# One core, a gated convolution and a mixture of experts: router logits computed with the operands swapped, and the statistics for a median measured and spread in another order

## The chip, the core and the metric

The kernel runs on one core of a Trainium2 chip. The metric is device time in microseconds (us), from one execution to the next of the same program. The engines are named as the profile names them: PE (TensorE, matmuls) with PEld (its weight loads), DVE (VectorE), ACT (ScalarE), POOL (GpSimd) and SP (SyncE, which only issues DMAs here). Each runs its own instructions in order, and they meet at semaphores.

## The reference, cut to what matters

The input is 8 images of 512 channels and 16 x 16 pixels, that is 2048 tokens of 512 channels.

```python
def conv(x):                                   # x: channel layer norm of the input, b c (h w)
    mean, mx, std = x.mean(-1), x.max(-1), x.std(-1, ddof=1)
    u = stack([mean, mx, std], -1)             # 8 x 512 x 3
    med = median(u.reshape(b, -1))             # one median of 1536 values for each image
    z = einsum('bck,ck->bc', (u - med)**3, cfc_w) / sqrt(1 + eps) * bn_w + bn_b
    return x * sigmoid(z)[:, :, None, None]
x = x + conv(ln_c(x))
def ffn(x):                                    # x: layer norm of a token
    logits = x @ router_w.T                    # 8 experts, the best one is taken
    top, idx = top_k(logits, 1)
    return sigmoid(top) * glu(x, w1[idx], v1[idx], w2[idx]) + glu(x, shared weights)
t = t + ffn(ln_t(t))
```

Every product is f32 and is made of three matmuls of type fp32r: each operand is split into a HI part and the rest, LO, and HI x HI, HI x LO and LO x HI are added.

## The kernel before, in words

**The stages.** (1) Up to about 41 us the 8 images ("batches" in the code, 256 tokens each) are normalized and turned so that channels lie on partitions; the turned batch `b` lies in two banks of the PSUM tile `GU`, two channel groups (k = 0, 1) in the first bank and two (k = 2, 3) in the second. Mean, maximum and standard deviation over its tokens are taken there: DVE measures the first bank with `bn_stats` and `bn_aggr` (L685, L693) and takes both maxima (L694, L696), ACT sums and squares the second bank (L513, L517), POOL makes the standard deviations (L391 to L394). (2) From 41 to 63 us the medians are found: the statistics are copied 16-fold into `scratch` (DVE L713 eight of twelve columns, ACT L537 four), turned by 12 transposes on PE (L1097) and one more (L1099) so that 1536 values of an image stand on each of its 16 partitions, and searched in 7 steps (L725 on DVE, L546 on ACT, each counting one half of the values; PE adds the counts). Before its first step ACT splits four pieces of the first weights (L532). Between the steps PE runs matmuls on ones, whose results nobody reads (L1071). (3) From 63 to 76 us the gates are made and applied to the first tiles. (4) From 76 to 203 us the 16 tiles of 128 tokens pass through the shared expert while the next tiles are prepared. (5) The tokens are sorted by expert, gathered and sent through the experts in blocks of 128.

**The loop of stage 4.** Its order is written out by hand: `PREPARED` names the tiles that each step n prepares (one, or two in steps 3 and 6). A step of PE is: gate product of tile n+1 (12 matmuls of 512 columns), transposes of the hidden tile n (L1148), up product of n+1, transposes of the next tile (`prepare`, L1141), down product of tile n into `yb`, routing of the prepared tile (L1187). Routing loads the tile's 128 x 128 HI and LO pieces as weights, eight in all, and moves the 16 columns of `router_parts` (HI and LO of 8 experts) through each; the logits of 128 tokens come out in `th` with tokens on partitions, and DVE copies them out (`keep_logits`, L806). `th` also holds the transposes of the hidden tile, so the two uses wait for one another. After the last tile DVE picks the experts (`choose`, L891 on).

**What the names are.** `means_kept`, `std_done`, `bank_measured`, `squares`, `spread_ready` and `spread_act` are the semaphores between stages 1 and 2. `y_used` tells that DVE has read `yb`. `xhi`, `xlo`, `hhi`, `hlo` tell that HI and LO of a turned tile are written. `SPLIT_AFTER` names the steps after which a third of the next weights is split (ACT L490, DVE L831).

Of the kernel before, what the change touches and what calls it, by code (L numbers as in the profile page):

```python
# [44 lines left out]
def program(nc, B, x_tok, conv_par, router, weights, xn_d, z_d, out):  # L45
# [12 lines left out]
    with ExitStack() as ctx:  # L58
# [36 lines left out]
        steps = sb("steps", [P, SEARCH_STEPS])  # L95
        conv = sb("conv", [P, KC * 5])
# [109 lines left out]
        logits = sem("logits")  # L206
        logits_used = sem("logits_used")
# [20 lines left out]

        def tally(i):

            return (yb, mb)[i % 2][:, i:i + 1]
# [10 lines left out]
        def stats_columns(of, to):  # L242

            return stats_rows[:, :, of:to].rearrange("p b s -> p s b").unsqueeze(3).to_broadcast([P, to - of, B, TPART])
# [92 lines left out]
        def _(pool):  # L337
# [50 lines left out]
            def channel_std(b):  # L388
# [3 lines left out]
                pool.wait_ge(bank_measured, 2 * b + 1)  # L392
# [95 lines left out]
        def _(act):  # L488
# [48 lines left out]
            act.activation(spread_rows(BY_COPY, KC * 3), stats_columns(BY_COPY, KC * 3), ACT.Copy).then_inc(spread_act, 1)  # L537
# [50 lines left out]
            silu_gate(0, 0)  # L588
            x_hi(2, 2)
            for n in range(NT - 1):  # L590
# [6 lines left out]
                for t in soon:  # L597
                    if t >= RING:
                        norm_a(t, t % RING)
                for t in now[1:]:  # L600
                    x_hi(t, t % RING)
                if n in SPLIT_AFTER:
                    k = SPLIT_AFTER.index(n)
                    act.wait_ge(w_in[k], 16 * 2)
                    split_hi(w_raw[:, k, :, :], w_parts[:, 1, k, HI, :, :])
            x_hi(NT, 0)
# [35 lines left out]
        def _(dve):  # L642
# [30 lines left out]

            def measure(tokens, channels):


                if tokens is not None:
                    dve.wait_ge(x_in[tokens], 16)
                    for h in range(2):
                        note(dve.bn_stats(bn_parts[:, h, :], x_sb[:, 2 * tokens + h, :]))  # L680
                if channels is not None:
                    aT = GU[:, 2 * (channels % 2):2 * (channels % 2) + 2, :].rearrange("p a (h t) -> p a h t", t=TPB)
                    dve.wait_ge(aT_ready, channels + 1)
                    for k in range(2):
                        note(dve.bn_stats(bn_parts[:, 2 + k, :], aT[:, 0, k, :]))  # L685
                settle()
                if tokens is not None:
                    for h in range(2):
                        note(dve.bn_aggr(tok_mv[:, 2 * tokens + h, :], bn_parts[:, h, :]))
                    dve.engine_nop().then_inc(stats_a, 1)  # L690
                if channels is not None:
                    for k in range(2):
                        note(dve.bn_aggr(stats[:, channels, k, 0:2], bn_parts[:, 2 + k, :]))  # L693
                    dve.tensor_reduce(stats[:, channels, 0:2, MAX], aT[:, 0, :, :], AX_X, ALU.max).then_inc(bank_measured, 1)  # L694
                    dve.wait_ge(squares, 2 * (channels + 1))
                    dve.tensor_reduce(stats[:, channels, 2:4, MAX], aT[:, 1, :, :], AX_X, ALU.max).then_inc(bank_measured, 1)  # L696
# [107 lines left out]
            def keep_logits(t, u):  # L804
                dve.wait_ge(logits, t + 1)
                dve.tensor_copy(logit_parts[:, t, :] if isinstance(t, int) else tile_of(logit_parts, t), th[:, 0:2 * E]).then_inc(logits_used, 1)  # L806
# [34 lines left out]
            keep_logits(0, 0)  # L841
            gated(0, 0)
            x_lo(2, 2)
            keep_logits(1, 1)
            for n, prepared in enumerate(PREPARED):
# [5 lines left out]
                norm_tile(first, first % RING)  # L851
                h_lo(n, n % 2)
# [4 lines left out]
                for t in held:  # L857
                    keep_logits(t, t % RING)
# [5 lines left out]
                keep_logits(first, first % RING)  # L864
# [24 lines left out]
            def choose():  # L889

                dve.wait_ge(logits_used, NT)  # L891
# [117 lines left out]
            n = len(PREPARED)  # L1009
            choose()  # L1010
# [54 lines left out]
        def _(pe):  # L1065
# [32 lines left out]

            pe.transpose(V[:, NV - BY_ACT:NV - BY_ACT + P], stats_rows[:, :, :].rearrange("p b r -> p (b r)"), ident[:, :]).then_inc(v_ready, 1)  # L1099
# [62 lines left out]
            def gate_product(n, slot, parity, q, before):  # L1162
# [3 lines left out]
                product(gu(parity, GATE), xT[:, slot], q, GATE).then_inc(g_done, 1)  # L1166
# [11 lines left out]
            def route(t, slot):  # L1178
# [4 lines left out]
                else:  # L1183
                    pe.wait_ge(logits_used, t)
# [24 lines left out]
            for n, prepared in enumerate(PREPARED):  # L1209
# [3 lines left out]
                pe.wait_ge(logits_used, first - len(held))  # L1213
# [36 lines left out]
            gate_product(n + 1, 0, 0, 0, 0)  # L1250
# [88 lines left out]
```

## Time and profile before

| | us |
|---|---|
| three runs | 424.27, 425.77, 425.97 (median 425.77) |
| the profiled execution | 425.56 |
| its span, first to last instruction | 423.6 |
| PE busy in the span | 385.3 (91%) |
| DVE, ACT, POOL busy | 258.9, 160.1, 135.2 |

The span is the time from the first to the last instruction on the trace; 1.96 us of the execution lie outside it. PE's busy share is an average: from 76 us on it is busy nearly all the time, before that it mostly waits.

### The profile page before, as it was taken

How to read it: one execution, taken by the hardware profiler on the slowest of the kernel's cores; microseconds unless marked ns; L12 is line 12 of the kernel's file. 1: busy time of each engine (PE TensorE's matmuls, PEld its weight loads, DVE VectorE, ACT ScalarE, POOL GpSimd, SP SyncE). 2: the span in 40 equal slices, each digit the busy share in tenths (PEclk: the TensorE clock that was granted, in tenths of full speed). 3: DMA queues.
4: the chain of work that ended last, by engine and by line, in shares of the span. 5: the costliest groups of instructions: out<-in, count | busy, mean ns of one | idle time of the engine just before them, and what ended most of it. 6: DMA issues, size and time to landing. Idle time of an engine off the chain costs nothing.

```text
span 423.6 us, 6668 instructions
## 1 busy us (share of the span) xinstructions
PE 385.3 (91%) x1920; PEld 313.0 (74%) x1921; DVE 258.9 (61%) x493; ACT 160.1 (38%) x265; POOL 135.2 (32%) x187
## 2 busy tenths in 40 slices
PE   1556766999999999999999999999999999999995
PEld 1444224888888888888888888888888888888883
DVE  5896776555584795575775557627546753776322
ACT  3887764122323522322112335435153634353210
POOL 6676841001010000003212034633425452345301
PEclk9999799999999999999999999999999999999999
DMA  7900221011121363122004085765626775652210
GB/s 287 406 5 2 99 100 50 26 50 51 50 76 50 107 216 150 51 91 108 26 26 124 26 319 193 262 230 195 231 84 256 258 241 190 233 197 71 74 45 29
DMA packets 15788, 55.96 MB, mean 132 GB/s; under 512 B 2575, under 2 KB 2575, under 8 KB 12304
## 3 DMA queue, kind: packets, MB, share of 16 engines
q1 hardware_dynamic: 10960, 40.93, 27.1%
q0 software_dynamic: 4800, 14.69, 9.7%
q8 instruction: 15, 0.25, 0.2%
q14 instruction: 13, 0.11, 0.1%
HBM read 43.02 MB, written 13.63 MB: 134 GB/s over the span
## 4 chain that ended last, share of the span: by engine, by line
PE 84%; DVE 6%; ACT 3%; issue 3%; POOL 2%; DMA 1%; DVEq 0%; POOLq 0%; ACTq 0%
PE GU L1156 47%; PE yb L1156 23%; PE th L1148 4%; PE tx L1141 4%; PE th L1187 3%; DVE search_junk L725 2%; DVE bn_parts L680 1%; ACT tiles L502 1%; POOL tok_rstd L385 1%; DMA x_sb<-x_tok 1%; PE mb L1156 1%; ACT scratch L513 1%; PE th L1071 1%; DVE bn_parts L685 1%; PE th L1134 1%
## 5 line engine op out<-in xcount | busy, mean ns | idle before, releaser
L1156 PE MATMUL GU<-w_parts,xT 128*128 (+1 forms) x864 | 213.8, 396 | 0.0
L1156 PEld LDWEIGHTS GU<-w_parts,xT 128*128 128x128 f32 x864 | 158.5, 188 | 32.0 <-issue 0.2
L1156 PE MATMUL yb<-w_parts,hT 128*128 (+1 forms) x420 | 102.7, 393 | 0.0
L573 ACT ACTIVATE hT<-th 128x512 fp32r<-128x512 f32 x36 | 21.6, 599 | 190.2 <-PE th L1148 190.2
L1156 PEld LDWEIGHTS yb<-w_parts,hT 128*128 128x128 f32 x420 | 77.8, 188 | 15.7
L440 POOL DMA_INDIRECT out<-x_sb,scatidx x20 | 37.3, 1865 | 92.8 <-DVE x_sb L1006 87.5
L831 DVE TENSOR_TENSOR w_parts<-w_raw,w_parts 128x2048 f32 (+1 forms) x24 | 54.9, 2288 | 6.8 <-issue 6.5
L816 DVE TENSOR_TENSOR hidden<-hidden,GU 128x512 f32<-128x512 f32 x36 | 24.8, 688 | 42.2 <-PE GU L1156 37.0
L490 ACT ACTIVATE w_parts<-w_raw 128x2048 f32 (+1 forms) x24 | 45.2, 1910 | 4.2 <-issue 4.1
L414 POOL TENSOR_TENSOR x_rstd<-x_mv,eps 128x1 f32<-128x1 f32 x16 | 3.3, 205 | 118.7 <-DVE x_mv L792 118.7
L810 DVE TENSOR_TENSOR hT<-th,hT 128x512 fp32r<-128x512 f32 x36 | 24.8, 688 | 24.5 <-ACT hT L573 24.5
L563 ACT ACTIVATE xT<-tx 128x512 fp32r<-128x512 f32 x36 | 21.4, 595 | 34.5 <-PE tx L1141 34.5
L1083 PE MATMUL GU<-ident,tiles 128*128 128x128 f32 x64 | 15.3, 423 | 20.7 <-ACT tiles L502 20.7
L1006 DVE SCALAR_TENSOR_TENSOR x_sb<-yb,slotinfo,x_sb 128x512 f32<-128x512 f32 x19 | 14.2, 749 | 26.5 <-PE yb L1156 23.7
L1083 PEld LDWEIGHTS GU<-ident,tiles 128*128 128x128 f32 x64 | 12.7, 224 | 22.6 <-issue 16.0
L435 POOL DMA_INDIRECT x_sb<-z_d,tokidx x20 | 19.5, 974 | 26.0 <-DMA z_d<-x_sb 20.2
L801 DVE TENSOR_TENSOR xT<-tx,xT 128x512 fp32r<-128x512 f32 x36 | 24.6, 683 | 4.2 <-ACT xT L563 4.2
L431 POOL DMA_INDIRECT tiles<-xn_d,tokidx x20 | 19.3, 964 | 22.3 <-DVE slotinfo L958 16.5
L1141 PE MATMUL tx<-ident,tiles 128*128 128x128 f32 x144 | 21.6, 273 | 2.0 <-DVE xT L801 2.0
L568 ACT ACTIVATE hidden<-GU 128x512 f32<-128x512 f32 x36 | 21.6, 600 | 2.1 <-PE GU L1156 2.1
L1148 PE MATMUL th<-ident,hidden 128*128 128x128 f32 x144 | 21.5, 272 | 0.0
L1148 PEld LDWEIGHTS th<-ident,hidden 128*128 128x128 f32 x144 | 17.8, 140 | 4.6
(203 smaller groups left out, 352.7 us busy)
## 6 DMA issues: line engine op xcount, KB each, us to landing
w_raw<-weights SPq DMA_DIRECT2D x27, 1024.0 KB, 5.4
x_sb<-x_tok SPq DMA_DIRECT2D x8, 512.0 KB, 7.4
xn_d<-tiles SPq DMA_DIRECT2D x16, 256.0 KB, 2.0
z_d<-x_sb SPq DMA_DIRECT2D x16, 256.0 KB, 2.0
tiles<-xn_d,tokidx POOLq DMA_INDIRECT x20, 4.5
x_sb<-z_d,tokidx POOLq DMA_INDIRECT x20, 5.3
out<-x_sb,scatidx POOLq DMA_INDIRECT x20, 7.4
conv<-conv_par SPq DMA_DIRECT2D x1, 10.0 KB, 9.9
```

What stands on the lines that cost most here:

```text
L440: pool.indirect_dma_start(out[:, :], rows(scatidx, b), zg[:, b % RING, :], None, bounds_check=T - 1, oob_is_err=False).then_inc(o_out[b % ...
L490: act.activation(hi, raw, ACT.Copy).then_inc(whi, 1)
L568: act.activation(hidden[:, parity, :], gu(parity, GATE), ACT.Silu).then_inc(silu, 1)
L573: act.activation(hT[:, parity, HI, :, :], th[:, :].rearrange("p (k t) -> p k t", k=KC), ACT.Copy).then_inc(hhi, 1)
L801: dve.tensor_tensor(xT[:, slot, LO, :, :], tx[:, :].rearrange("p (k t) -> p k t", k=KC), xT[:, slot, HI, :, :].bitcast(F32), ALU.subtract) ...
L810: dve.tensor_tensor(hT[:, parity, LO, :, :], th[:, :].rearrange("p (k t) -> p k t", k=KC), hT[:, parity, HI, :, :].bitcast(F32), ALU.subtr ...
L816: dve.tensor_tensor(hidden[:, parity, :], hidden[:, parity, :], gu(parity, UP), ALU.mult).then_inc(hid_ready, 1)
L831: dve.tensor_tensor(lo, w_raw[:, k, :, :], hi.bitcast(F32), ALU.subtract).then_inc(wlo, 1)
L1083: last = pe.transpose(aT[:, k, h * P:(h + 1) * P], tiles[:, t % RING, k * P:(k + 1) * P], ident[:, :])
L1141: last = pe.transpose(tx[:, k * P:(k + 1) * P], src[:, k * P:(k + 1) * P], ident[:, :])
L1148: last = pe.transpose(th[:, k * P:(k + 1) * P], hidden[:, parity, k * P:(k + 1) * P], ident[:, :])
L1156: last = pe.matmul(dst, left[:, lp, kc, :], wset(q, k, wp, kc), start=(i == 0), stop=(i == 3 * KC - 1))
```

## The change

It has two parts that do not touch one another.

**Routing swapped.** Now `router_parts` (16 columns) is the weight and the tile's piece, 128 columns, is moved through it. The logits come out in `th` with the 16 (expert, part) rows on partitions and tokens along the columns. ACT copies these 16 x 128 values to `logits_T` (two slots of SBUF), PE transposes them back to 128 x 16 into `yb` in the next step (`turn_logits`; the last one into `tx`, in the middle of a gate product), and DVE takes all tiles of a step with one copy (`take_logits`). In the diff, `keep_logits` is a function of ACT's program now, `take_logits` one of DVE's.

```diff
+        logits_T = search_junk[0:2 * E, 0:2 * P].rearrange("p (a c) -> p a c", a=2)
...
-                        last = pe.matmul(th[:, 0:2 * E], xT[:, slot, lp, kc, :], router_parts[:, kc, :, :].rearrange("p h e -> p (h e)"),
+                        last = pe.matmul(th[0:2 * E, 0:P], router_parts[:, kc, :, :].rearrange("p h e -> p (h e)"), xT[:, slot, lp, kc, :],
...
+            def turn_logits(n, bank):
+                for i, t in enumerate(routed_in(n - 1)):
+                    pe.wait_ge(logits_kept, t + 1)
+                    pe.transpose(bank[:, i * 2 * E:(i + 1) * 2 * E], logits_T[:, t % 2, :], ident[0:2 * E, 0:2 * E]).then_inc(logits_turned, 1)
...
                 gate_product(n + 1, (n + 1) % RING, (n + 1) % 2, 0, 0)
-                pe.wait_ge(logits_used, first - len(held))
+                if n:
+                    pe.wait_ge(y_used, n)
+                turn_logits(n, yb)
                 transpose_h(n, n % 2)
...
+                pe.wait_ge(logits_used, n + 1)
                 down_product(n, n % 2, 0, 0)
...
-            gate_product(n + 1, 0, 0, 0, 0)
-            pe.wait_ge(logits_used, NT)
+            gate_product(n + 1, 0, 0, 0, 0, lambda: turn_logits(n, tx))
...
+            def keep_logits(t):
+                act.wait_ge(logits, t + 1)
+                act.activation(logits_T[:, t % 2, :], th[0:2 * E, 0:P], ACT.Copy).then_inc(logits_kept, 1)
...
+            def take_logits(n, bank):
+                tiles_in = routed_in(n - 1)
+                first, many = tiles_in[0], len(tiles_in)
+                dve.wait_ge(logits_turned, tiles_in[-1] + 1)
+                dve.tensor_copy(logit_parts[:, first:first + many, :],
+                                bank[:, 0:many * 2 * E].rearrange("p (t e) -> p t e", t=many)).then_inc(logits_used, 1)
...
                 norm_tile(first, first % RING)
+                take_logits(n, yb)
                 h_lo(n, n % 2)
```

On PE, one step of the loop of stage 4 (step 1), before:

```order
L1187 MATMUL th<-router_parts,xT 128x16 x8
L1156 MATMUL GU<-w_parts,xT 128x512 x12
L1148 MATMUL th<-ident,hidden 128x128 x4
L1156 MATMUL GU<-w_parts,xT 128x512 x12
L1141 MATMUL tx<-ident,tiles 128x128 x4
L1156 MATMUL yb<-w_parts,hT 128x512 x12
```

and the same step now (`search_junk` is the memory in which `logits_T` lies):

```order
L1232 MATMUL th<-xT,router_parts 16x128 x8
L1201 MATMUL GU<-w_parts,xT 128x512 x12
L1240 MATMUL yb<-ident,search_junk 128x16
L1193 MATMUL th<-ident,hidden 128x128 x4
L1201 MATMUL GU<-w_parts,xT 128x512 x12
L1186 MATMUL tx<-ident,tiles 128x128 x4
L1201 MATMUL yb<-w_parts,hT 128x512 x12
```

The eight routing matmuls stand where they stood, now writing 16 x 128, and one small transpose per tile has come in ahead of the transposes of the hidden tile. Steps that route two tiles have two.

**The last two batches by bank, and the spread by kind.** For batches 6 and 7 DVE now measures the first bank of both and only then takes the maxima of the second banks, which wait for ACT's squares. The spread is by kind: the four maxima (DVE), the four means (DVE), the four standard deviations (ACT), and PE transposes in that order; it waits for the standard deviations only ahead of the last transpose.

```diff
-            for b in range(B + 2):
-                measure(b if b < B else None, b - 2 if b >= 2 else None)
+            for b in range(B):
+                measure(b, b - 2 if b >= 2 else None)
+            for b in (B - 2, B - 1):
+                first_bank(b)
+            for b in (B - 2, B - 1):
+                second_bank(b)
+            settle()
...
-            dve.wait_ge(std_done, B)
+            dve.tensor_copy(spread_rows(0, KC), stats_plane(MAX)).then_inc(spread_ready, 1)
             dve.wait_ge(means_kept, 1)
-            dve.tensor_copy(spread_rows(0, BY_COPY), stats_columns(0, BY_COPY)).then_inc(spread_ready, 1)
+            dve.tensor_copy(spread_rows(KC, 2 * KC), stats_plane(MEAN)).then_inc(spread_ready, 1)
...
-                pool.wait_ge(bank_measured, 2 * b + 1)
+                pool.wait_ge(bank_measured, 2 * b + (1 if b < B - 1 else 0))
...
-            act.activation(spread_rows(BY_COPY, KC * 3), stats_columns(BY_COPY, KC * 3), ACT.Copy).then_inc(spread_act, 1)
+            act.activation(spread_rows(BY_COPY, KC * 3), stats_plane(STD), ACT.Copy).then_inc(spread_act, 1)
...
-            pe.wait_ge(means_kept, 1)
-            pe.wait_ge(std_done, B)
+            pe.wait_ge(squares, 2 * B)
             pe.wait_ge(bank_measured, 2 * B)
...
-                if s == 0:
-                    pe.wait_ge(spread_ready, 1)
+                if s in (0, KC):
+                    pe.wait_ge(spread_ready, 1 + s // KC)
...
+            pe.wait_ge(std_done, B)
             pe.transpose(V[:, NV - BY_ACT:NV - BY_ACT + P], stats_rows[:, :, :].rearrange("p b r -> p (b r)"), ident[:, :]).then_inc(v_ready, 1)
```

On DVE, from batch 6 to the copies for the spread, before:

```order
L685 BN_STATS bn_parts<-GU 128x6 x2
L693 BN_AGGR stats_rows<-bn_parts 128x2 x2
L694 TENSOR_REDUCE stats_rows<-GU 128x2
L696 TENSOR_REDUCE stats_rows<-GU 128x2
L685 BN_STATS bn_parts<-GU 128x6 x2
L693 BN_AGGR stats_rows<-bn_parts 128x2 x2
L694 TENSOR_REDUCE stats_rows<-GU 128x2
L696 TENSOR_REDUCE stats_rows<-GU 128x2
L704 CAST router_parts<-router_w 128x4x8
L705 TENSOR_TENSOR router_parts<-router_w,router_parts 128x4x8
L710 TENSOR_SCALAR stats_rows<-neg_mean 128x8x2
L713 COPY scratch<-stats_rows 128x1024
```

and now:

```order
L706 BN_STATS bn_parts<-GU 128x6 x2
L709 BN_AGGR stats_rows<-bn_parts 128x2 x2
L710 TENSOR_REDUCE stats_rows<-GU 128x2
L706 BN_STATS bn_parts<-GU 128x6 x2
L709 BN_AGGR stats_rows<-bn_parts 128x2 x2
L710 TENSOR_REDUCE stats_rows<-GU 128x2
L716 TENSOR_REDUCE stats_rows<-GU 128x2 x2
L748 CAST router_parts<-router_w 128x4x8
L749 TENSOR_TENSOR router_parts<-router_w,router_parts 128x4x8
L754 TENSOR_SCALAR stats_rows<-neg_mean 128x8x2
L755 COPY scratch<-stats_rows 128x512
L757 COPY scratch<-stats_rows 128x512
```

The two maxima of second banks (L696 before, L716 now) have moved behind both first banks, and one copy of 1024 columns has become two of 512.

## Rows read from the trace of the kernel before

**Rows 1.** The page: busy time of each engine, and the chain by engine.
```profile
PE 385.3 (91%) x1920; PEld 313.0 (74%) x1921; DVE 258.9 (61%) x493; ACT 160.1 (38%) x265; POOL 135.2 (32%) x187
...
PE 84%; DVE 6%; ACT 3%; issue 3%; POOL 2%; DMA 1%; DVEq 0%; POOLq 0%; ACTq 0%
```

**Rows 2.** Busy time by stretch: from:to, length, engines, granted clock, DMA.
```profile
39.00:41.00 2.00, 0.03 (x1) 0.01 (x1) 1.45 (x6) 0.77 (x2) 1.06 (x2) 1.00 0.00 0
...
41.50:47.50 6.00, 4.59 (x19) 2.48 (x18) 3.33 (x12) 4.59 (x10) 6.00 (x5) 0.50 0.07 10
...
62.50:65.00 2.50, 2.50 (x10) 1.70 (x9) 0.46 (x4) 0.23 (x1) 0.00 (x0) 0.50 0.00 0
...
76.00:196.00 120.00, 120.00 (x641) 100.93 (x639) 74.79 (x132) 34.77 (x52) 9.89 (x27) 1.00 0.24 88
```

**Rows 3.** The chain in order of time: start, us, what; two routings, two expert blocks.
```profile
91.63 0.79 PE th L1187 x8
...
101.71 0.79 PE th L1187 x8
...
242.92 2.72 PE GU L1156 x12
...
251.98 2.73 PE GU L1156 x12
```

**Rows 4.** PE's timeline in step 1: start, us, engine, line, operation, form.
```profile
87.74 1.04 PE L1187 MATMUL th<-router_parts,xT 128*128 128x16 f32 x8
88.64 2.99 PE L1156 MATMUL yb<-w_parts,hT 128*128 128x512 f32 x12
...
95.15 0.60 PE L1148 MATMUL th<-ident,hidden 128*128 128x128 f32 x4
95.50 3.02 PE L1156 MATMUL GU<-w_parts,xT 128*128 128x512 f32 x12
...
98.71 3.00 PE L1156 MATMUL yb<-w_parts,hT 128*128 128x512 f32 x12
```

**Rows 5.** Copies beside the loop: ACT's 256-column copies, DVE's LO of step 1.
```profile
L513 ACT ACTIVATE scratch<-GU 128x256 f32<-128x256 f32 x16 | 5.8, 366 | 0.0
...
96.43 0.68 DVE L810 TENSOR_TENSOR hT<-th,hT 128x512 fp32r<-128x512 f32 x1
```

**Rows 6.** The timeline in step 6, the wait ahead of the second prepared tile.
```profile
153.39 0.42 PEld L1141 LDWEIGHTS tx<-ident,tiles 128*128 128x128 f32 x4 [0.42 <-DVE tiles L797]
```

**Rows 7.** The timeline from batch 7 to the search's first step; idle before and releaser.
```profile
35.80 3.23 PE L1071 MATMUL th<-ones_bf 128*128 128x512 bf16 x9
...
37.05 0.75 DVE L685 BATCH_NORM_STATS2 bn_parts<-GU 128x6 f32<-128x256 f32 x2
...
38.00 0.66 DVE L694 TENSOR_REDUCE stats_rows<-GU 128x2 f32<-128x512 f32 x1
38.28 0.22 POOL L391 TENSOR_SCALAR z<-z 128x2 f32<-128x2 f32 x1 [0.15 <-ACT scratch L517]
38.58 0.68 DVE L696 TENSOR_REDUCE stats_rows<-GU 128x2 f32<-128x512 f32 x1
38.82 0.22 POOL L393 TENSOR_SCALAR z<-stats_rows 128x2 f32<-128x2 f32 x1 [0.32 <-DVE stats_rows L694]
39.12 1.03 POOL L394 TENSOR_TENSOR stats_rows<-z,powers 128x4 f32<-128x4 f32 x1
...
40.18 0.69 DVE L713 COPY scratch<-stats_rows 128x1024 f32<-128x1024 f32 x1 [0.51 <-POOL stats_rows L394]
40.23 0.63 ACT L537 ACTIVATE scratch<-stats_rows 128x512 f32<-128x512 f32 x1 [2.03 <-POOL stats_rows L394]
40.76 2.17 ACT L532 ACTIVATE w_parts<-w_raw 128x512 fp32r<-128x512 f32 x4
...
41.02 2.38 PE L1097 MATMUL GU<-ident,scratch 128*128 128x128 f32 x12 [1.99 <-DVE scratch L713]
...
43.65 0.90 ACT L546 ACTIVATE scratch<-GU,search 128x768 f32<-128x768 f32 x1 [0.71 <-PE GU L1099]
```

More of the change, by code:

```diff
@@ L206, in program @@
         logits = sem("logits")
+        logits_kept = sem("logits_kept")
+        logits_turned = sem("logits_turned")
         logits_used = sem("logits_used")
@@ L227, in gate_rows, with routed_in @@
             return w_raw[:, DOWN, batch - STORED_GATES.start, :] if batch in STORED_GATES else mb[:, :]
+        def routed_in(n):
+            if n < 0:
+                return (0, 1)
+            held = PREPARED[n - 1][1:] if n else (2,)
+            return held + PREPARED[n][:1]
         def tally(i):
@@ L588, in _ @@
             silu_gate(0, 0)
+            keep_logits(0)
             x_hi(2, 2)
+            keep_logits(1)
             for n in range(NT - 1):
@@ L599, in _ @@
                         norm_a(t, t % RING)
+                if now:
+                    for t in routed_in(n)[:-1]:
+                        act.wait_ge(logits_turned, t - 1)
+                        keep_logits(t)
                 for t in now[1:]:
@@ L605, in _ @@
                     split_hi(w_raw[:, k, :, :], w_parts[:, 1, k, HI, :, :])
+                for t in now[:1]:
+                    act.wait_ge(logits_turned, t - 1)
+                    keep_logits(t)
             x_hi(NT, 0)
@@ L671, in _, with banks, first_bank, second_bank @@
             own(dve.memset(search[:, 0:1], SEARCH_FROM))
+            def banks(b):
+                return GU[:, 2 * (b % 2):2 * (b % 2) + 2, :].rearrange("p a (h t) -> p a h t", t=TPB)
+            def first_bank(b):
+                dve.wait_ge(aT_ready, b + 1)
+                for k in range(2):
+                    note(dve.bn_stats(bn_parts[:, 2 + k, :], banks(b)[:, 0, k, :]))
+                settle()
+                for k in range(2):
+                    note(dve.bn_aggr(stats[:, b, k, 0:2], bn_parts[:, 2 + k, :]))
+                dve.tensor_reduce(stats[:, b, 0:2, MAX], banks(b)[:, 0, :, :], AX_X, ALU.max).then_inc(bank_measured, 1)
+                settle()
+            def second_bank(b):
+                dve.wait_ge(squares, 2 * (b + 1))
+                dve.tensor_reduce(stats[:, b, 2:4, MAX], banks(b)[:, 1, :, :], AX_X, ALU.max).then_inc(bank_measured, 1)
             def measure(tokens, channels):
[L677 to L680, printed above, removed]
+                dve.wait_ge(x_in[tokens], 16)
+                for h in range(2):
+                    note(dve.bn_stats(bn_parts[:, h, :], x_sb[:, 2 * tokens + h, :]))
                 if channels is not None:
-                    aT = GU[:, 2 * (channels % 2):2 * (channels % 2) + 2, :].rearrange("p a (h t) -> p a h t", t=TPB)
                     dve.wait_ge(aT_ready, channels + 1)
                     for k in range(2):
-                        note(dve.bn_stats(bn_parts[:, 2 + k, :], aT[:, 0, k, :]))
+                        note(dve.bn_stats(bn_parts[:, 2 + k, :], banks(channels)[:, 0, k, :]))
                 settle()
[L687 to L690, printed above, removed]
+                for h in range(2):
+                    note(dve.bn_aggr(tok_mv[:, 2 * tokens + h, :], bn_parts[:, h, :]))
+                dve.engine_nop().then_inc(stats_a, 1)
                 if channels is not None:
@@ L863, in _ @@
                 add_shared(n)
-                keep_logits(first, first % RING)
             def carve(space, at, *widths):
@@ L1009, in _ @@
             n = len(PREPARED)
+            take_logits(n, tx)
             choose()
@@ L1160, in product, with gate_product @@
                 return last
-            def gate_product(n, slot, parity, q, before):
+            def gate_product(n, slot, parity, q, before, amid=None):
                 pe.wait_ge(wlo, before + 1)
                 pe.wait_ge(xlo, n + 1)
-                product(gu(parity, GATE), xT[:, slot], q, GATE).then_inc(g_done, 1)
+                product(gu(parity, GATE), xT[:, slot], q, GATE, amid).then_inc(g_done, 1)
             def up_product(n, slot, parity, q, before):
```

21 lines of the change are left out of this document (7 added, 14 removed).

## The prediction, made before the changed kernel ran

> **What bounds the kernel now.** I read the page first. PE has by far the most work and holds 84% of the chain that ended last [rows 1], so a change counts where it takes work off PE or shortens what PE waits for. Busy time by stretch tells where which holds: from 76 to 196 us PE is busy for all of 120 us at a granted clock of 1.00, while ACT is busy for 35 of them and DVE for 75 [rows 2]. There every us of PE work is a us of the kernel. Between 39 and 41 us PE does nothing [rows 2]; the timeline shows it waiting for DVE's copy of the statistics, which waits for POOL's standard deviations [rows 7]. The change touches one place of each kind.
>
> **Routing, what it costs now.** In the chain one routing of a tile takes 0.79 us [rows 3]. That is a low figure, since the load that the next product waits for shows there. From the first routing matmul to the first of the next product it is 88.64 - 87.74 = 0.90 us for eight pairs of load and matmul, 0.112 us a pair [rows 4]. As a bound from above: a step with a routing takes 101.71 - 91.63 = 10.08 us, an expert block with the same three products and eight transposes, but no routing, 251.98 - 242.92 = 9.06 [rows 3]; 1.02 us is the most that one can lay on it. I take 0.90, for 16 tiles 14.4 us.
>
> What sets the 0.112 us? A product matmul that moves 512 columns takes 2.72 / 12 = 0.227 us [rows 3], so 16 columns would stream in 0.007. A transpose, which moves 128 columns but also loads 128 weight columns, goes at (95.50 - 95.15) / 4 = 0.088 us at least [rows 4]. Pairs that move 16 and 128 columns take about the same time; what they share is the load of 128 columns. So routing is bound by its weight loads, and the swap takes the load from 128 columns to 16. The Trainium skill says the same in "TensorE: Matmul & The Clock Gate", section "LDWEIGHTS (loading the stationary operand)": load time goes with the number of weight columns, P / 1.2 ns. By it 128 columns take 107 ns, which the 0.112 agrees with, and 16 would take 13 (an estimate); no row here shows so narrow a load.
>
> **Routing, what it will cost.** The eight matmuls now move 128 columns each. From below, by the product's pace: 0.227 / 4 = 0.057 us. From above, by the transposes' and the routing's own pace: 0.112. I take 0.062, near the lower end, since what holds the pace at the upper end is the wide load, which is gone. The product's first load (128 columns) can hide only behind the last routing matmul, so that one counts as 0.11: 7 x 0.062 + 0.11 = 0.55 us, bounds 0.51 and 0.90. New is the transpose back: it loads 128 columns from 16 partitions and moves 16, so like a routing pair of today: 0.11 us. Saved per tile: 0.90 - 0.55 - 0.11 = 0.24 us, bounds +0.28 and -0.11.
>
> One tile's saving is lost. In step 6, which prepares two tiles, PE already waits 0.42 us for DVE to normalize the second one [rows 6]. DVE's chain up to there starts with a transposed tile of step 5 and is not shorter than before: one copy of logits goes, `take_logits` comes. The routing of step 5 and the transpose of step 6 lie between; what PE saves there becomes a longer wait, 0.66 us. So 15 x 0.24 = 3.6 us, bounds -1.7 and +4.2.
>
> **What lies beside.** ACT gets 16 copies of 16 x 128. Its copies of 256 columns take 0.366 us [rows 5], so 0.37 each is a bound from above and 5.9 us in all; ACT has 85 idle us in the stretch [rows 2]. In its queue a copy stands behind the routing it waits for and ahead of the HI copy of the next hidden tile, which PE makes ready one gate product (2.7 us) later. PE's new wait for `y_used` ahead of `turn_logits` asks that DVE has added the previous down product; that add follows the product at once, and PE gets there a gate product later. `take_logits` stands ahead of `h_lo` on DVE; in step 1 `h_lo` ends at 97.1 and the down product that needs it starts at 98.71 [rows 4, 5], so 1.6 us cover some 0.2. On the other hand DVE no longer waits for the end of each routing. After the last tile the logits reach DVE half a gate product (1.4 us) later; PE needs the choice of experts, a few small operations of DVE, only two products (5.4 us) after the last routing, so I cost this at nothing; without that cover it would be the 1.4 us.
>
> **The statistics.** Batch 7 has been transposed when PE starts its filler matmuls at 35.80, but DVE measures it only from 37.05, behind the second-bank maximum of batch 6 [rows 7]. Now it starts at about 36.0 and the first-bank maximum (38.00 now) is there at 37.0 to 37.7. POOL then waits only for ACT's squares: L391 at 38.28, L393 0.30 behind it (as L394 is behind L393) at 38.58 instead of 38.82, the power 0.24 us earlier, its end at 39.91 instead of 40.15. The second-bank maximum of batch 7 starts at 38.3 instead of 38.58 and ends at 39.0; three small operations follow as before, then two copies, each about half of the 0.69 us of L713: an estimate of 39.75 for the maxima and 40.1 for the means. So PE starts at about 39.75 instead of 41.02, 1.27 us earlier, and no longer waits for POOL with its first eight transposes. Its 2.63 us up to the first counting pass (43.65 - 41.02) then end at 42.4.
>
> What is late next is ACT. It copies the standard deviations when POOL is done, from 39.99, then runs four weight pieces of 2.17 us, and only then can it count: 40.76 + 2.17 = 42.93 now, 42.7 after. Each search step needs both halves. So the first step starts at 42.7 on ACT instead of 43.65: 0.95 us, bounds 0.24 (POOL's gain alone) and 1.27. From there to 76 us the chain through search and gates is the same, only earlier.
>
> **The sum.** 425.56 - 0.95 - 3.6 = 421.0 us, against the profiled execution; the median of the runs, 425.77, lies 0.2 above it.
>
> **What the clock does.** The granted clock is 1.00 from 39 to 41 us, 0.50 (1.2 GHz) from 41.5 to 47.5 after PE's idle stretch, and again 0.50 from 62.5 to 65, after the sparse matmuls of the median's end [rows 2]. In the second stretch PE is busy for all 2.5 us, on filler and gate transposes that gate the first tiles; at 2.4 GHz half of that would do. So where a fall lies can move the kernel by about 1.3 us either way; my bounds take that in.
>
> **The rivals.** (a) *A pair keeps its price.* If a pair costs 0.112 us whatever the width of its load, eight pairs still take 0.90 and the transposes back come on top: 15 x 0.11 = 1.7 us more, and 425.56 - 0.95 + 1.7 = 426.3. For it: only loads of 128 columns are in the trace. Against it: the product's load hides behind its matmul entirely, so a pair isn't a fixed price.
>
> (b) *Narrow fp32r matmuls take four passes.* The trace shows one pass for 512 columns (0.227 us), and for 16 columns it can't tell: four passes would be 0.028 us, hidden under 0.112. At four passes 128 columns take 0.227 us, eight 1.82, and with the transpose a tile is slower by 1.82 + 0.11 - 0.90 = 1.03 us: 425.56 - 0.95 + 16 x 1.03 = 441. It decides from two passes on: 0.114 us is rival (a). Against it: nothing in the products hints at a slower form. The Trainium skill, "FP8 and Floating Point Precision", section "TensorE Precision Notes", has true FP32 as four passes and a reduced-precision read that truncates; the products' pace agrees with the second, and the page names no limit on width.
>
> (c) *DVE takes over.* With PE shorter per step, DVE's chain (wait of step 6, two tiles in step 3) could hold PE at more places. Half of the routing's saving would go: 425.56 - 0.95 - 1.8 = 422.8. Against it: DVE is busy for 75 of 120 us [rows 2].
>
> (d) *The statistics give nothing,* because something behind them (the first weights on POOL, a clock fall that comes earlier) is late anyway: 425.56 - 3.6 = 422.0.
>
> **Chances and range.** Forecast 0.64, its own range 419.3 to 422.6; (a) 0.10; (b) 0.12; (c) 0.08; (d) 0.06. The range from 419.2 to 426.4 leaves out (b) and tails of the forecast. A measurement of this kernel tells about 0.5% (2.1 us) from no change: below 423.6 is faster. That holds for the forecast, (c) and (d): 0.77 with a little off for the tail; (a) and the tail are the same, 0.11; (b) is slower, 0.12.
>
> **What would show it.** Right: routing matmuls about 0.06 us apart and about 0.5 us a tile in the chain; one extra transpose a tile of about 0.11; a step at about 9.84 us; the wait in step 6 at about 0.66; PE's first spread transposes at 39.8, the first counting pass at 42.7, with ACT's weight pieces ending last before it. Wrong: 1.8 us a tile (b), 0.9 (a), new waits of PE on DVE or ACT between 76 and 196 us (c), a median that ends no earlier (d).

## The result, and the profile after

The changed kernel takes 422.78 us (median of six runs, 422.25 to 423.08), the kernel before, run beside it, 425.63 (six runs, 424.27 to 425.97). The gain is 2.85 us (0.7%) by the medians and 2.65 by the profiled executions (425.56 to 422.91, spans 423.6 to 421.0). The ratio on record, 0.995 [0.9934, 0.9966], isn't that of the medians (0.9933); by it the gain is 0.5%, about 2.1 us. Forecast were 4.6 us. The direction was right and the time lies in the range, just above the forecast's own (419.3 to 422.6), but more than a third of the gain is missing by the medians and more than half by the ratio.

The page after the change, busy time and the chain by engine, against [rows 1]:

```profile
PE 381.9 (91%) x1933; PEld 306.4 (73%) x1937; DVE 258.6 (61%) x490; ACT 163.5 (39%) x281; POOL 135.1 (32%) x187
...
PE 80%; DVE 8%; ACT 4%; issue 3%; POOL 3%; DMA 1%; DVEq 0%; POOLq 0%; ACTq 0%
```

PE lost 3.4 us of work and still holds most of the chain that ended last.

Busy time by stretch, the columns as in [rows 2]; the number ahead of the DMA share is the granted clock:

```profile
41.50:47.50 6.00, 3.00 (x10) 0.80 (x10) 4.28 (x14) 5.31 (x12) 6.00 (x6) 0.76 0.14 19
...
62.50:65.00 2.50, 1.97 (x14) 1.27 (x14) 1.73 (x3) 0.70 (x2) 0.00 (x0) 1.00 0.00 0
72.00:75.00 3.00, 3.00 (x9) 2.35 (x8) 2.21 (x5) 0.30 (x1) 0.73 (x2) 0.50 0.00 0
76.00:196.00 120.00, 119.91 (x668) 97.02 (x666) 74.83 (x129) 38.27 (x68) 9.49 (x26) 1.00 0.25 89
```

Two things are to be seen. From 76 us on PE is as full as before, so its work still is time. And the stretch at 1.2 GHz that lay at 62.5 to 65 us [rows 2] lies at 72 to 75 in this execution, where PE is busy for all three us.

The timeline from the spread of the standard deviations to the first gate product, against [rows 7] (start, length, instruction, and in brackets the idle time before it):

```profile
38.79 1.16 POOL L404 TENSOR_TENSOR stats_rows<-z,powers 128x4 f32<-128x4 f32 x1
...
39.72 1.66 PE L1141 MATMUL GU<-ident,scratch 128*128 128x128 f32 x12 [0.85 <-DVE scratch L755]
40.03 0.63 ACT L547 ACTIVATE scratch<-stats_rows 128x512 f32<-128x512 f32 x1 [1.93 <-POOL stats_rows L404]
40.57 2.17 ACT L542 ACTIVATE w_parts<-w_raw 128x512 fp32r<-128x512 f32 x4
...
42.65 0.88 ACT L556 ACTIVATE scratch<-GU,search 128x768 f32<-128x768 f32 x1
...
71.42 4.57 PE L1201 MATMUL GU<-w_parts,xT 128*128 128x512 f32 x12
```

PE starts its spread transposes at 39.72 and ACT its first counting pass at 42.65, both within 0.1 us of the forecast. The last four of its twelve transposes, those of the standard deviations, wait for ACT's copy of them (`spread_act`), so PE depends on POOL there already and not only ahead of its last transpose. But the first gate product takes 4.41 us from its start to the routing behind it (75.83); at 2.4 GHz it takes 2.84, so 1.57 us go to the low clock there.

The chain of waits in steps 1 and 2, against [rows 3] (start, length, what):

```profile
90.31 0.48 PE th L1232 x8
90.78 2.81 PE GU L1201 x12
93.60 0.22 PE yb L1240 x2
93.82 0.59 PE th L1193 x4
94.41 2.76 PE GU L1201 x12
...
100.38 0.48 PE th L1232 x8
100.86 2.81 PE GU L1201 x12
103.67 0.16 PE yb L1240
103.83 0.59 PE th L1193 x4
...
110.35 0.48 PE th L1232 x8
```

Routing is 0.48 us a tile in the chain, where it was 0.79 [rows 3]. But the step became 110.35 - 100.38 = 9.97 us, where it was 10.08 and the forecast had 9.84. What routing saved went to the turn, the transpose back (L1240): 0.16 us itself, and 0.59 for the hidden transposes behind it, which take 0.44 where nothing stands ahead of them.

### The profile page after: what moved, and what is told of

Read it like the earlier page. It is cut to its first block, busy times and chain, and to the rows that moved or that the text cites. A ratio compares the mean times of both kernels' runs of the same rounds, so it can differ in the third digit from the quotient of the medians.

```text
span 421.0 us, 6721 instructions
## 1 busy us (share of the span) xinstructions
PE 381.9 (91%) x1933; PEld 306.4 (73%) x1937; DVE 258.6 (61%) x490; ACT 163.5 (39%) x281; POOL 135.1 (32%) x187
## 4 chain that ended last, share of the span: by engine, by line
PE 80%; DVE 8%; ACT 4%; issue 3%; POOL 3%; DMA 1%; DVEq 0%; POOLq 0%; ACTq 0%
PE GU L1201 46%; PE yb L1201 21%; PE th L1193 4%; PE tx L1186 4%; PE th L1232 2%; DVE search_junk L769 1%; DVE bn_parts L722 1%; POOL tok_rstd L395 1%; DMA x_sb<-x_tok 1%; POOL stats_rows L404 1%; ACT tiles L512 1%; PE mb L1201 1%; PE th L1179 1%; ACT w_raw L594 1%; ACT scratch L523 1%
## 5 line engine op out<-in xcount | busy, mean ns | idle before, releaser
L869 DVE TENSOR_TENSOR x_sb<-x_sb,yb 128x512 f32<-128x512 f32 x16 | 11.0, 686 | 15.8 <-PE yb L1201 15.7
```

## Experiments

Three theories were on trial. A: the turn costs some 0.31 us a place instead of 0.11 because of its shape, 16 partitions. B: the statistics' gain is lost to where the stretches at 1.2 GHz fall. C, formed after the first eight runs: at full clock ACT's four weight pieces end last ahead of the first counting pass with either statistics, so there is no gain to lose. In the expectations of the first six runs A and B are letters of each run's own; from the filled kernels on they are these. The kernel before measured 424.71, 424.65 and 424.74 us beside the three groups of four runs, so times of these groups can be compared. Beside the changed kernel it measured 425.63, 0.9 us more, so a distance from the changed kernel's 422.78 is less certain; routing alone, measured in the first group, stands beside it below.

### Statistics alone, routing alone

The first has the new statistics on the kernel before, the second the new routing.

> The statistics' half of the change alone, routing as before. Theory A: the half does what was forecast up to the first counting pass (42.7 instead of 43.65 us) but shifts the stretch in which the granted clock falls, from about 62 us to about 72 us, into the first gate product; then of the 0.95 us some 0.5 is left: a kernel time of 424.9 to 425.3. Rival B: the clock does not depend on this half, the 0.95 us arrive whole: 424.5 to 424.8.

Measured: 424.87 us (423.34 to 425.78), ratio 0.9993 [0.9978, 1.0009]. The median lies between the two expectations. In the profiled execution the first gate product ran at full clock (1.00 from 72 to 75 us), so the fall into it, the mechanism of this run's theory A, was not seen.

> The routing's half alone, statistics as before. Theory A: the eight swapped matmuls save what was forecast (0.36 us a tile), but each of the 12 places where logits are turned back costs about 0.31 us (two tiles at one place 0.37) instead of 0.11 a tile, since PE does not overlap the small transpose with its neighbours; saved in all about 2.0 us: 423.5 to 423.9. Rival B, my forecast of 3.6 us holds for this half and the change's shortfall comes from the statistics: 421.8 to 422.3.

Measured: 422.68 us (422.55 to 423.55), ratio 0.9945 [0.9928, 0.9962]. The median lies between the two expectations; its 2.0 us against the kernel before beside it (424.71) and the span's last part (350.0 to 348.0, table below) are the 2.0 us of theory A. By the medians the routing half alone is the whole change, and the statistics half is worth nothing that can be measured.

### The turn on 128 partitions

```diff
-logits_T = search_junk[0:2 * E, 0:2 * P]...
+logits_T = search_junk[:, 0:2 * P]...
-pe.transpose(bank[:, i * 2 * E:(i + 1) * 2 * E], logits_T[:, t % 2, :], ident[0:2 * E, 0:2 * E])
+pe.transpose(bank[:, i * P:(i + 1) * P], logits_T[:, t % 2, :], ident[:, :])
```

Nothing waits for anything else than in the changed kernel; only the shape differs: 128 partitions instead of 16, and 128 moved columns instead of 16 (112 of the 128 columns that come out are not used).

> The changed kernel, but each transpose of logits takes all 128 partitions of its slot (16 hold logits, the others old finite numbers that nobody reads on) and moves 128 columns, like PE's other transposes; all waits stay as they are. Theory A: the gap at each of the 12 places comes from the 16-partition shape; it goes, a place costs 0.11 us (two tiles 0.22), and the time is 2.0 to 2.5 us below the changed kernel's: 420.3 to 420.8. Rival B: the gap comes from the waits on the load of that transpose (yb read, logits kept), which are the same; then nothing changes or it gets slower by the longer moving: 422.6 to 423.3.

Measured: 420.46 us (419.2 to 420.85), ratio 0.9882 [0.9861, 0.9903]: 2.3 us below the changed kernel, 2.2 below routing alone. Its chain in step 2:

```profile
99.67 0.48 PE th L1232 x8
100.15 2.82 PE GU L1201 x12
102.97 0.11 PE yb L1240
103.08 0.44 PE th L1193 x4
103.51 2.77 PE GU L1201 x12
...
109.47 0.48 PE th L1232 x8
```

The turn is 0.11 us, the hidden transposes are back at 0.44, and the step is 9.80 us. The load that goes with the turn, from the timeline of the changed kernel:

```profile
93.53 0.20 PEld L1240 LDWEIGHTS yb<-ident,search_junk 16*128 16x128 f32 x2 [0.35 <-issue]
```

The engine of the loads stood idle for 0.35 us ahead of it. And from the timeline of this kernel:

```profile
92.66 0.37 PEld L1240 LDWEIGHTS yb<-ident,search_junk 128*128 128x128 f32 x2
```

No bracket, no idle time. With 16 partitions the idle stands at each of the 12 places (4.2 us in all), and the profile shows nothing that it waits for. Theory A holds: a load of eight times the rows is the cheaper one. It isn't the small number of moved columns: the routing pairs of before moved 16 columns behind loads of 128 partitions at 0.112 us a pair [rows 4]. Nor is it a narrow load by itself: the routing loads now have 16 columns, from 128 partitions, and no idle time stands ahead of them. How many partitions are enough was not tried.

### Filler ahead of the first gate product

```diff
 prepare(0)
+keep_warm(6, yb)
 prepare(1)
```

> The changed kernel with six filler matmuls on ones (1.3 us at 2.4 GHz) between the transposes of tiles 0 and 1, where PE idles for about two us. Theory A: the clock's fall into the first gate product (4.33 us instead of 2.75 in the profile) goes, and the time is 1.0 to 1.6 us below the changed kernel's: 421.2 to 421.8. Rival B: the fall is an accident of the profiled execution, or comes elsewhere: no change, 422.5 to 423.1.

Measured: 421.83 us (421.31 to 422.5), ratio 0.9921 [0.9902, 0.994]. In the profiled execution, by stretch:

```profile
60.00:64.00 4.00, 4.00 (x16) 2.33 (x14) 1.78 (x8) 0.23 (x1) 0.00 (x0) 0.61 0.00 0
72.00:75.00 3.00, 2.90 (x15) 2.52 (x16) 2.69 (x5) 0.60 (x1) 0.49 (x2) 1.00 0.01 3
```

The gate product runs at full clock, and the low stretch is back at 60 to 64. Three of the six runs lie at 421.31 to 421.38, the others at 422.28 to 422.5, where this execution is. That the filler saves 1.0 us by the medians fits theory B; that the low clock only moved in this execution made it clear that single executions have to be taken apart before they are compared.

### One turn for four tiles

```diff
-act.activation(logits_T[0:2 * E, t % 2, :], th[0:2 * E, 0:P], ACT.Copy)
+act.activation(logits_T[32 * (t % 4):32 * (t % 4) + 2 * E, t // 4 % 2, :], th[0:2 * E, 0:P], ACT.Copy)
...
+if g is None:
+    return
+pe.transpose(bank[:, 0:P], logits_T[:, g % 2, :], ident[:, :])
```

> The changed kernel with the logits of four tiles kept on four strips of 32 partitions and turned back by one 128x128 transpose for four tiles: 4 such transposes instead of 16, and a step between them has none. With full-height transposes a turn measured 0.108 us beside its neighbours. Theory A (each turn costs PE what the trace shows, and nothing else hangs on it): 12 turns x 0.108 = 1.3 us less than the kernel with one 128-row turn for each tile (420.46): 419.2. Rival (the place between gate product and hidden transposes costs something by itself, the copies to strips and the larger take are later): within 0.4 us of it, 420.1 to 420.9.

Measured: 419.88 us (419.53 to 420.77), ratio 0.9883 [0.9863, 0.9904]. By its median it lies between the two: 0.6 us below the kernel with a turn for each tile. But the part of the span from the first gate product on fell from 346.0 to 344.9 us (table below), 1.1 of the 1.3 us expected; of the rest 0.04 is what step 6 waits longer for DVE (0.73 against 0.69 us).

### Old and new statistics under the same routing

> The kernel before with the routing half alone, the turn on 128 partitions; the statistics stay as before. Against it the run with both halves and the same turn measured 420.46. Theory A (the turn's shape was the whole loss of the routing half): 12 places x 0.2 us = 2.4 us below the routing half with 16-row turns (422.68): 420.3 to 420.6, about the same as both halves, since the statistics half measured 424.87 against 424.71. Rival (the statistics half is worth its 0.95 us, and the medians of single runs hid it by where the low clock fell): 421.3 to 421.6, 0.9 to 1.1 us above both halves.

Measured: 421.04 us (419.39 to 421.74), ratio 0.9905 [0.988, 0.9931]. Between the two theories by its median, and its runs lie 1.1 us apart in three places. The timeline of this kernel, which has the statistics of the kernel before:

```profile
40.81 1.50 PE L1122 MATMUL GU<-ident,scratch 128*128 128x128 f32 x12 [2.62 <-DVE scratch L737]
...
42.15 0.27 PE L1124 MATMUL GU<-ident,stats_rows 128*128 128x128 f32 x1
42.47 1.02 DVE L749 TENSOR_SCALAR_CACHE_REDUCE search_junk<-GU,search 128x768 f32<-128x768 f32 x1 [1.68 <-PE GU L1124]
42.64 0.88 ACT L556 ACTIVATE scratch<-GU,search 128x768 f32<-128x768 f32 x1
```

By stretch, the granted clock again ahead of the DMA share:

```profile
38.00:41.00 3.00, 0.38 (x3) 0.22 (x3) 2.24 (x7) 0.98 (x2) 1.47 (x3) 1.00 0.00 0
41.00:43.00 2.00, 1.43 (x13) 1.19 (x11) 0.54 (x1) 2.00 (x5) 1.75 (x2) 1.00 0.03 8
```

The same two places with routing alone, the same statistics, in an execution whose granted clock was 0.50 from 42 to 46 us:

```profile
40.83 2.60 PE L1122 MATMUL GU<-ident,scratch 128*128 128x128 f32 x12 [2.09 <-DVE scratch L737]
...
43.68 0.90 ACT L556 ACTIVATE scratch<-GU,search 128x768 f32<-128x768 f32 x1 [0.93 <-PE GU L1124]
```

These rows decide the case. With the old statistics ACT counts at 42.64 in the one and at 43.68 in the other, as it did at 43.65 in the trace of before [rows 7]. The transposes start at the same time; they take 1.50 us at full clock, 2.60 here and 2.38 before [rows 7] in a stretch at 0.50 [rows 2]. The new statistics reach 42.65. So the 0.95 us was the price of a stretch at 1.2 GHz, not of the statistics' order. This is theory C. The runs agree: the one of this kernel at a mean granted clock of 1.00 took 419.39 us, the two lowest with the new statistics 419.2 and 419.36.

### Both with PE's idle stretches filled

```diff
-keep_warm(9)
+keep_warm(14)
...
+keep_warm(8)
...
-keep_warm(4)
+keep_warm(7)
```

The first edit stands ahead of the spread transposes (19 with the old statistics), the second behind them, the third in each counting pass; 2, 4, 5 and 6 more follow behind the passes.

> Both halves with 128-row turns, and PE's idle stretches from 36 to 72 us filled with matmuls on ones whose result nobody reads (5 more ahead of the spread transposes, 8 behind them, 3 more in each of seven counting passes, 2, 4, 5 and 6 more behind them). Theory B (the stretches of low granted clock between 38 and 76 us take away what the statistics win): no stretch at half clock is left where PE is waited for, the times lie in one cluster at or below the lowest of the unfilled kernel (419.2): 418.2 to 419.3. Rival (the filling delays what is waited for, or the clock falls all the same): 419.5 or above.

Measured: 419.33 us (419.3 to 419.5), ratio 0.9868 [0.9847, 0.989], at the upper end of what theory B expected.

> The kernel before with the routing half alone and 128-row turns, with the same filling of PE's idle stretches (10 more ahead of the spread transposes, which start later here). Theory B (with the clock at its full level in both, the statistics half is worth what its chain shows, 43.65 against 42.65 us for the first counting pass): 0.9 to 1.1 us above the filled kernel with both halves. Rival (the statistics half brings nothing even at full clock, because something behind the first counting pass is waited for anyway): within 0.3 us of it.

Measured: 420.12 us (419.58 to 421.45), ratio 0.9894 [0.987, 0.9917], 0.8 us above the one before by the medians. The filling works: from 41 to 76 us the granted clock is 1.00 in both profiles, and the runs with both halves lie within 0.2 us; those with the old statistics don't (three lie at 420.6 to 421.45). As a test of the statistics it is half spoiled: ahead of the spread transposes the clock was low in the first kernel's profile, 14 fillers took 5.22 us, and the transposes waited for them until 40.71. ACT counted at 42.58 and 42.72 in the two profiles. The three lowest runs of the old statistics (419.58 to 419.64) lie 0.1 to 0.3 us above the new, which is nearer to the rival's price than to theory B's.

### Two weight pieces ahead of the first pass instead of four

```diff
-EARLY_HI = 4
+EARLY_HI = 2
```

The two others follow behind the last counting pass. If theory C holds, this uncovers the gain of the statistics.

> Both halves with 128-row turns, and ACT copies 2 instead of 4 weight pieces ahead of the first counting pass; the two others follow behind the last pass, where ACT waits 3.45 us. Theory C (at full clock ACT's four weight pieces, 40.59 to 42.67, end last ahead of the first pass with either statistics, so that the statistics half is hidden behind them): the first pass starts at 41.6 instead of 42.67, and the time falls by about 1.0 us against the kernel with four (420.46): 419.4, lowest runs near 418.2. Rival (the medians' later waits, or where the clock falls, take it back): 420.0 to 420.8.

Measured: 419.41 us (419.16 to 419.97), ratio 0.9877 [0.9854, 0.99], as expected by the median; no run came near the 418.2 expected of the lowest.

> The routing half with 128-row turns on the kernel before's statistics, with 2 weight pieces ahead of the first pass. Theory C: the spread transposes end at 42.4 at full clock, the first pass starts at 42.5 instead of 42.64: 0.1 to 0.2 us below the same kernel with four pieces (421.04), and 0.9 us above the one with both halves and two pieces: the statistics half is then worth what the prediction gave it. Rival (the statistics half is worth nothing here either): within 0.3 us of the kernel with both halves and two pieces.

Measured: 420.38 us (420.19 to 421.44), ratio 0.9902 [0.9881, 0.9924]: 0.97 us above the one before, and 0.7 below the same kernel with four pieces, where 0.1 to 0.2 was expected. The timeline with the new statistics:

```profile
40.50 1.13 ACT L542 ACTIVATE w_parts<-w_raw 128x512 fp32r<-128x512 f32 x2
...
41.14 0.27 PE L1144 MATMUL GU<-ident,stats_rows 128*128 128x128 f32 x1
...
41.54 0.88 ACT L556 ACTIVATE scratch<-GU,search 128x768 f32<-128x768 f32 x1
```

ACT goes from its two pieces to the count without a wait. The timeline with the old ones:

```profile
40.53 1.14 ACT L542 ACTIVATE w_parts<-w_raw 128x512 fp32r<-128x512 f32 x2
...
42.13 0.27 PE L1124 MATMUL GU<-ident,stats_rows 128*128 128x128 f32 x1
42.44 0.90 ACT L556 ACTIVATE scratch<-GU,search 128x768 f32<-128x768 f32 x1 [0.77 <-PE GU L1124]
```

With the cover gone, the pass starts 0.90 us earlier with the new statistics, and the old ones now wait for PE. Theory C holds on both sides, and with two pieces the new statistics are 0.97 us faster than the old. In both profiles the part from there to the gate product is the same (29.90 and 29.92, table below), so the low clock doesn't make this difference.

### The best of all

> Both halves, one 128x128 turn for four tiles, and 2 weight pieces ahead of the first counting pass. Theory: the two savings lie in different stages and add: 419.88 less 1.0 for the pieces, 418.9, lowest runs near 418.3. Rival (the turn for four tiles waits for a later tile's logits, and the first pass's gain is lost to the clock's fall): 419.5 or above.

Measured: 418.35 us (417.5 to 419.74), ratio 0.9857 [0.9832, 0.9882], a little below what was expected.

> As the one before, with PE's idle stretches behind the spread transposes filled with matmuls on ones that nobody reads (5 behind the transposes, 7 instead of 4 in each counting pass, 2, 4, 5 and 6 more behind them), and none more ahead of them, where the filled kernels ran 14 to 19 of them to 40.9 us and kept the transposes waiting. Theory: no stretch at 1.2 GHz between 41 and 76 us, one narrow cluster of times at 417.8 to 418.6. Rival (the clock falls all the same, or the filling is in the way): as the unfilled kernel or above.

Measured: 417.27 us (417.18 to 417.38), ratio 0.9824 [0.9801, 0.9846], all five runs within 0.2 us, and a little below what was expected. Both halves of the change with one turn for four tiles, two early pieces and filled stretches are 7.5 us below the kernel before measured beside it, and 5.5 below the changed one's 422.78. Its stretches:

```profile
36.00:41.00 5.00, 4.47 (x18) 2.13 (x18) 3.93 (x13) 3.04 (x12) 3.06 (x6) 0.70 0.00 0
41.00:46.00 5.00, 4.47 (x24) 1.92 (x23) 3.83 (x12) 4.31 (x9) 4.62 (x4) 1.00 0.01 3
46.00:60.00 14.00, 12.50 (x59) 4.79 (x59) 11.06 (x47) 11.29 (x22) 10.39 (x9) 1.00 0.40 150
60.00:64.00 4.00, 3.27 (x21) 1.88 (x19) 2.59 (x8) 0.87 (x3) 0.00 (x0) 1.00 0.00 0
```

From 36 to 76 us the clock is low only between 36 and 41, where PE ran filler until the spread transposes; these started at 39.79 and took 1.65 us, as in the kernels whose clock is full there.

### The spans taken apart

The span of each profiled execution cut at two instructions, ACT's first counting pass and the first gate product (from the timelines; us):

| kernel | first pass | to the gate product | from there to the end |
|---|---|---|---|
| before | 43.65 | 29.93 | 350.0 |
| changed | 42.65 | 28.77 | 349.6 |
| statistics alone | 42.51 | 29.68 | 350.1 |
| routing alone | 43.68 | 29.93 | 348.0 |
| turn on 128 partitions | 42.67 | 29.90 | 346.0 |
| filler at 72 us | 42.57 | 29.91 | 348.0 |
| one turn for four | 42.67 | 29.92 | 344.9 |
| old statistics, 128 partitions | 42.64 | 29.90 | 346.0 |
| both filled | 42.58 | 28.80 | 346.0 |
| old statistics filled | 42.72 | 28.81 | 346.2 |
| two pieces, new statistics | 41.54 | 29.90 | 346.1 |
| two pieces, old statistics | 42.44 | 29.92 | 346.0 |
| four turns, two pieces | 41.63 | 28.76 | 345.0 |
| the same, filled | 41.68 | 28.80 | 344.8 |

The last column is the routing alone, within 0.2 us: 350.0 with the old, 348.0 with turns on 16 partitions, 346.0 with 128, 344.9 with one for four. (The changed kernel's 349.6 are 348.0 and the 1.57 that the low clock took from its first gate product.) The middle column has two values: 28.8 where the clock is full from 60 to 68 us, 29.9 where a low stretch lies in there (29.68 once). A low stretch in the counting passes alone costs nothing that shows: the changed kernel had 0.76 from 41.5 to 47.5 us and 28.77 in this column. The first column is the statistics, the number of weight pieces and the low clock on the spread transposes. The time of a run is the sum and 1.9 to 2.1 us around the span.

## Why the prediction was right and wrong

**What bounds the kernel: right.** PE's work from 76 us on is time; three shapes of the turn moved the last part by about what they cost PE.

**Routing itself: right.** From the first start of the eight matmuls to the next product it is 90.62 - 90.14 = 0.48 us, where 0.55 was forecast; that is 0.06 us for each of them (forecast 0.062, and 0.11 for the last). The records, by line:

```profile
L1232 PEld LDWEIGHTS th<-xT,router_parts x128: 92/96/99, 75.6 to 193.8; 128*16 128x16 f32 x128
L1232 PE MATMUL th<-xT,router_parts x128: 218/223/305, 75.8 to 193.8; 128*16 128x128 f32 x128
```

Rival (a) with its fixed price of 0.112 us a pair and rival (b) with four passes are out. The rule drawn on, the Trainium skill's "TensorE: Matmul & The Clock Gate", section "LDWEIGHTS (loading the stationary operand)", pointed the right way; the 13 ns that its formula gives for 16 columns (an estimate) can't be read here, as a load of 16 columns is recorded with 96 ns in a pair that takes 60.

**The step that failed: "like a routing pair of today: 0.11 us" for the transpose back.** The term was mis-sized. That price was taken from loads with 128 partitions, and the turn loads from 16. In the changed kernel a place with one turn costs PE 0.31 us by the starts of the timeline: about 0.09 ahead of it, 0.16 itself, 0.06 behind it. A place with two turns costs 0.37, where 0.22 was forecast. On eight places of the one kind and four of the other that is 8 x 0.20 + 4 x 0.15 = 2.2 us more than forecast; in step 6 the wait for DVE is shorter by 0.17 for it, which leaves 2.0. The run with 128 partitions got back 2.3 by the medians and 2.0 by the span's last part. The wait in step 6 in the changed kernel:

```profile
151.45 0.42 PEld L1186 LDWEIGHTS tx<-ident,tiles 128*128 128x128 f32 x4 [0.52 <-DVE tiles L841]
```

and with 128 partitions:

```profile
150.06 0.42 PEld L1186 LDWEIGHTS tx<-ident,tiles 128*128 128x128 f32 x4 [0.69 <-DVE tiles L841]
```

With 128 partitions the forecast's own numbers came out, or nearly so: the turn at 0.11, a step of 9.80 us (9.84 forecast), a wait in step 6 of 0.69 (0.66 forecast), and a gain of 4.0 us in the last part, where 3.6 was forecast with a bound of 4.2. Only the number of columns was weighed. The Trainium skill has a rule that speaks against the small shape, on the page "TensorEngine Tiling (Array Packing)", section "Key Properties": changing the tiling mode of the array drains the engine. The idle 0.35 us of the load engine ahead of the load at each place with 16 partitions, and none with 128, would agree with it; but the page doesn't say that a load from 16 partitions is another mode, it gives no price, and no run here shows the drain itself.

**The statistics: the second step that failed, "So the first step starts at 42.7 on ACT instead of 43.65: 0.95 us".** Each place of the new order came as forecast: PE at 39.72, ACT at 42.65, the weight pieces last. But the 43.65 from which 0.95 us was reckoned held a stretch at 1.2 GHz. The prediction had read that stretch [rows 2], but priced only the second one, at 62.5 us, as a shift of 1.3 us either way, and carried the length that the transposes had in the first one (its 2.63 us) over to the new kernel. At full clock the old statistics let ACT count at 42.64 in the run above, behind its weight pieces, with PE done at 42.4: the term is about nothing. The prediction's lower bound, 0.24 for POOL's gain, was nearest, and even of that little arrived: from POOL's first operation on batch 7 (L391 before, L401 now) to ACT's copy it is 1.95 us before and 1.85 now, as the power takes 1.16 us where it took 1.03 [rows 7]. A term of nothing is rival (d), with the cover that the prediction itself had named ("what is late next is ACT"); it was given a chance of 0.06. The kernel before without a low stretch comes to 42.64 + 28.8 + 350.0 + 1.9 = 423.3 us, and its runs at a mean granted clock of 0.999 took 423.39 to 423.56; the changed one comes to 42.65 + 28.8 + 348.0 + 1.9 = 421.3. None of its own six runs is there (422.25 is the lowest); the lowest of the kernel with filler at 72 us is 421.31. So at full clock the change is worth an estimated 2.0 us, all of it routing. That the two profiled executions lie 2.65 us apart is in good part luck: 1.0 us up to the first pass and 1.2 from there to the gate product are low stretches that the one had there and the other hadn't, and of routing's 2.0 us the low clock on the first gate product took 1.57 back.

**Beside it: right.** Rival (c) didn't come about, though the 422.8 that it gave is the measured time: that is accident. DVE held PE in step 6 alone, as before, and ACT's sixteen copies (busy for 38.3 us of the 120, from 34.8) held up nothing.

What stays open: what the load engine does in the idle 0.35 us, and why the low stretch falls where it does in one execution and elsewhere in the next. PE's idle time alone doesn't say it: after 2.09 us of it the spread transposes ran into a stretch at 0.50, after 2.62 they ran at 1.00, with the same statistics. No profile of the new statistics shows these transposes at low clock (1.47 to 1.66 us), so an order that starts them earlier may still be spared that price at times; the medians of single runs don't show it. Its prices are known (1.0 us on the spread transposes, 1.1 near 60 us, 1.57 on the first gate product), and filling PE's idle time removed it from the stretch where they are paid.

## What to carry to other kernels

Before a gain is read from a stretch, look at its granted clock: what a low clock lengthens there is not the work's own cost, and the chain has to be worked out again at full clock, where another engine may end last. Price a small matmul by all its sizes, partitions too: padded to 128 partitions, or gathered until it fills them, it can be cheaper than alone. Where times lie in clusters, cut the spans at two or three instructions and compare the parts, since the medians mix them.

## What was not expected of the hardware

- A transpose of 16 partitions among matmuls of 128 cost 0.31 us a place, the same with 128 partitions 0.11, and one of 128 partitions did the work of four for the same 0.11.
- Matmuls on ones that nobody reads, in PE's idle time, lowered the time: 418.35 to 417.27 us, and the spread of the runs from 2.2 to 0.2 us.
- One stretch at 1.2 GHz can be worth as much as a change: the same first gate product took 2.84 and 4.41 us.
